# Two attention layers on one core: maxima of scores taken over two PSUM banks at once, scores in three single banks, and two of the three relative-position sets done as one

## The reference, cut to what matters

```python
# x: (16, 32, 32, 192) float32; 12 heads of 16; S = 32*32 = 1024
x = x + L0(_gn(x))     # _gn: group norm, 32 groups
x = x + L1(_gn(x))

def L0(x):             # global attention with decomposed relative positions
    q, k, v = split(x @ w_qkv.T + b_qkv)              # per head (S, 16)
    r_q = q.reshape(heads, H, W, 16)
    rel_h = einsum('bhwc,hkc->bhwk', r_q, Rh)         # Rh, Rw: (32, 32, 16)
    rel_w = einsum('bhwc,wkc->bhwk', r_q, Rw)
    bias = (rel_h[..., :, None] + rel_w[..., None, :]).reshape(heads, S, S)
    attn = softmax(q @ k.T * 16 ** -0.5 + bias)       # 1024 x 1024 per head
    return (attn @ v) @ w_proj.T + b_proj

def L1(x):             # 7x7 neighbourhood attention with 16 register keys
    scores = where(mask_cat, q @ concat(k, reg_k).T / 4, -1e30)
    return (softmax(scores) @ concat(v, reg_v)) @ out_w.T + out_b
```

## Time and profile before

| | |
|---|---|
| median of 3 runs | 4869.27 us (4869.14 to 4873.89) |
| profiled execution | 4862.39 us, span 4860.6 us |
| granted clock of TensorE, mean | 0.967 |
| TensorE busy | 4446.6 us, 91% of the span |
| VectorE busy | 3079.8 us, 63% |
| ScalarE busy | 2594.1 us, 53% |
| GpSimd busy | 892.4 us, 18% |

### The profile page before, as it was taken

One profiled execution on the slowest core, in us unless ns is written; L12 is line 12 of the kernel. 1 busy time (PEld: TensorE's weight loads), 2 busy tenths in 40 slices (PEclk: granted clock), 3 DMA queues, 4 the chain that ended last, 5 costly groups with the idle time before them and its releaser, 6 DMA issues.

```text
span 4860.6 us, 97545 instructions
## 1 busy us (share of the span) xinstructions
PE 4446.6 (91%) x32598; PEld 2268.6 (47%) x32598; DVE 3079.8 (63%) x5558; ACT 2594.1 (53%) x3955; POOL 892.4 (18%) x1901
## 2 busy tenths in 40 slices
PE   4879999999999999999999999999999999999988
PEld 3334453544535454453544535454453544535434
DVE  3736667666675756657566675756757566675644
ACT  1533556555564655555555565555546555565564
POOL 4122021222202222021222202222031221202111
PEclk7988999999999999999999999999999999999999
DMA  6333152442514433153442424433253432424402
GB/s 123 87 73 77 44 119 64 100 87 56 107 42 107 88 89 75 44 115 68 100 80 58 101 52 103 91 83 75 45 114 75 100 80 49 103 60 100 88 15 40
DMA packets 235869, 386.05 MB, mean 79 GB/s; under 512 B 58396, under 2 KB 133728, under 8 KB 235360
## 3 DMA queue, kind: packets, MB, share of 16 engines
q1 hardware_dynamic: 189280, 266.13, 23.7%
q10 hardware_dynamic: 21504, 75.51, 7.8%
q0 software_dynamic: 24576, 37.80, 4.9%
HBM read 227.79 MB, written 88.08 MB: 65 GB/s over the span
## 4 chain that ended last, share of the span: by engine, by line
PE 71%; DVE 11%; issue 6%; DMA 5%; SPq 5%; ACT 2%; DVEq 0%; ACTq 0%; POOL 0%
PE P L1143 14%; PE P L1161 13%; PE P L1102 12%; DVE mx L909 7%; PE P L966 5%; PE P L967 5%; PE P L1193 4%; PE P L1214 4%; DMA queries<-oraw 4%; PE P L1110 3%; PE P L1079 3%; SPq L514 3%; DVE mxc L915 2%; PE P L1186 1%; PE P L1231 1%
## 5 line engine op out<-in xcount | busy, mean ns | idle before, releaser
L909 DVE TENSOR_REDUCE mx<-P 128x1 f32<-128x512 f32 x3072 | 1921.3, 684 | 457.4 <-PE P L1102 453.3
L779 ACT ACTIVATE probs<-P 128x1024 f32<-128x1024 f32 x1536 | 1507.5, 1022 | 854.0 <-PE P L1161 853.8
L1102 PE MATMUL P<-K,AR 96*128 96x256 f16 x6144 | 1074.1, 278 | 56.6 <-DMA AR<-biases 29.5
L1161 PE MATMUL P<-AR,K 113*128 113x512 f16 x3072 | 924.9, 383 | 13.2 <-DMA AR<-mrow 12.6
L915 DVE TENSOR_REDUCE mxc<-P 128x1 f32<-128x336 f32 (+1 forms) x1536 | 656.3, 474 | 317.9 <-PE P L1111 315.0
L1143 PE MATMUL P<-probs,V 128*17 128x512 f32 x6144 | 813.5, 601 | 5.7 <-ACT probs L779 5.7
L1102 PEld LDWEIGHTS P<-K,AR 96*128 96x128 f16 x6144 | 532.2, 98 | 581.4 <-DVE mx L909 202.0
L795 ACT ACTIVATE probs<-P 128x320 f32<-128x320 f32 (+3 forms) x1632 | 612.1, 437 | 338.2 <-PE P L1214 268.4
L1161 PEld LDWEIGHTS P<-AR,K 113*128 113x128 f16 x3072 | 213.3, 98 | 670.3 <-ACT probs L779 519.6
L1110 PE MATMUL P<-K,A 112*128 112x320 f16 (+1 forms) x1536 | 405.2, 300 | 68.7 <-DVE mx L909 54.9
L1214 PE MATMUL P<-A,K 113*128 113x320 f16 (+2 forms) x1536 | 428.3, 300 | 14.7 <-ACT probs L795 14.3
(11 more groups left out here) (125 smaller groups left out, 3718.4 us busy)
## 6 DMA issues: line engine op xcount, KB each, us to landing
AR<-biases SPq DMA_DIRECT2D x384, 256.0 KB, 7.9
AR<-queries ACTq DMA_DIRECT2D x96, 512.0 KB, 5.9
biases<-xn SPq DMA_DIRECT2D x128, 256.0 KB, 2.6
AR<-queries ACTq DMA_DIRECT2D x96, 256.0 KB, 8.8
K<-oraw POOLq DMA_DIRECT2D x384, 64.0 KB, 4.7
xin<-in_x_dram SPq DMA_DIRECT2D x16, 768.0 KB, 10.5
queries<-oraw SPq DMA_DIRECT2D x384, 32.0 KB, 4.6
QA<-queries SPq DMA_DIRECT2D x192, 64.0 KB, 2.8
```

The costliest lines, as they stand in the source:

```text
L779: nc.scalar.activation(probs[:, u % RING, j:j + 2, :], P[:, b:b + 2, :], ACT.Exp).then_inc(p_done[0], 1)
L909: V_.reduce_max(mx[:, n // 2, n % 2:n % 2 + 1], bank, AX.X).then_inc(used, 1)
L1102: last = mm(bank[:, QD * (v % 2):QD * (v % 2) + QD], AR[0:ROWS_MAX[0], part % SLOTS, v, c, j, 128 * q:128 * q + 128], K0[0:ROWS_MAX[0], h, ...
L1161: last = mm(P[:, j, :], K0[0:ROWS, h, 128 * kt:128 * kt + 128], AR[0:ROWS, p % SLOTS, kt // 2, :, j, :], start=True, stop=True)
```

## The change

- L0 maxima in main0: a job is now a pair (`max2`): four matmuls into two neighbouring banks, one maximum over 1,024 columns, written straight to `mxc`; L912 and its semaphore are not used there. L1 maxima in main0 are pairs too: two tiles of equal width (`TILE_PAIRS`), one instruction with two results. In main1 they stay single.
- Job banks in main0: 3, 4, 5, 6 in place of 4, 5, 7. A pair takes two that begin at an even place of the ring; a transpose or stat takes one, and the next pair skips what is left of its two. Values go to bank 7.
- Scores in main0: three single banks; ScalarE takes each by itself (two exponentials of 512 in place of one of 1,024), and semaphores count singles.
- Relative positions: sets 1 and 2 are done together in main1 at steps 9 to 23 of every second step, eight jobs of 4 lines, two matmuls a line of 128 columns. Their parts are kept in `oraw` and `xin`, so ScalarE waits before it writes `oraw` again, and SP before it loads `xin`. Main0 has none. `QA` holds three sets; set 2's queries are fetched right behind set 1's.
- The wait for ones in row 96 of `xn` in L0's `out` is gone.

```diff
-RELS = 4
+RELS = 4, 8
-SCORES, JOBS = (4, 3), 3
-JOB_BANKS = ((4, 5, 7), (3, 4, 5))
+SCORES = 3
+JOB_BANKS, VALUES_BANK = ((3, 4, 5, 6), (3, 4, 5)), 7
+SINGLES = 2 * STEPS[0]
+TILE_PAIRS = ((0, 7), (1, 2), (3, 4), (5, 6))
...
+def max_pairs(layer, image, part):
+
+    return [("max2", layer, image, part, n) for n in range(0, ITEMS[layer] + 1, 2)]
...
-        before = jobs[len(jobs) - JOBS] if len(jobs) >= JOBS else None
-        after[place].append((len(jobs), job, before))
+        wide = 1 + (job[0] == "max2" and job[4] < ITEMS[job[1]])
+        at += at % wide
+        taken = [ring[(at + k) % len(ring)] for k in range(wide)]
+        before = max((held[b] for b in taken if b in held), default=None)
+        after[place].append((taken[0], job, None if before is None else jobs[before]))
+        for b in taken:
+            held[b] = len(jobs)
         jobs.append(job)
+        at += wide
...
-    placed += [(8 + 3 * n, job) for n, job in enumerate(rel_jobs(image, 2))]
...
-    placed += [(8 + 2 * n, job) for n, job in enumerate(rel_jobs(n0, 1))]
+    placed += [(9 + 2 * n, job) for n, job in enumerate(rel_jobs(n0, 1))]
...
                 query_blocks(im, 1)
+                query_blocks(im, 2)
...
                     fill_slot(image, part)
-                    if part == 2:
-                        query_blocks(image, 2)
...
+            def rel_moved():
+
+                while staged:
+                    image = staged.pop()
+                    for g in (1, 2):
+                        act.wait_ge(biases_out[g], (image + 1) * PER_BIASES)
...
-                        act.wait_ge(st_done[0], im * STEPS[0] + step + 1)
-                        b = 2 * (step % 2)
-                        nc.scalar.activation(probs[:, u % RING, j:j + 2, :], P[:, b:b + 2, :],
-                                             ACT.Exp).then_inc(p_done[0], 1)
+                        for k in range(2):
+                            single = 2 * step + k
+                            act.wait_ge(st_done[0], im * SINGLES + single + 1)
+                            nc.scalar.activation(probs[:, u % RING, j + k, :], P[:, single % SCORES, :],
+                                                 ACT.Exp).then_inc(p_done[0], 1)
...
+                        elif what == "max2" and layer == 0:
+                            V_.reduce_max(mxc[0][:, n // 2:n // 2 + 1], banks(at, 2), AX.X).then_inc(used, 2)
+                        elif what == "max2":
+                            (a, b), h = TILE_PAIRS[n % TT // 2], n // TT
+                            lo, hi = key_rows(a)
+                            V_.tensor_reduce(mxc[1][:, TT * h + a:TT * h + b + 1:b - a],
+                                             P[:, at:at + 2, 0:W * (hi - lo) + REG], AX.X, ALU.max).then_inc(used, 2)
...
+                    q = QA[:, sets[0]:sets[1], :, :].rearrange("p g h (l w) -> p (g h) l w", w=16)
+                    table, cols = n * lines // 16, 512 // lines
+                    for b in range(lines):
+                        line = n * lines % 16 + b
                         rhs = q[:, :, :, line] if table else q[:, :, line, :]
...
-                            last = mm(bank[:, 64 * b:64 * b + 64], lhs, rhs, start=(s == 0), stop=(s == 1))
+                            last = mm(bank[:, cols * b:cols * b + cols], lhs, rhs, start=(s == 0), stop=(s == 1))
...
                         for j in (2 * k, 2 * k + 1):
-                            h = GH * (p // 2) + j
-                            last = mm(P[:, j, :], K0[0:ROWS, h, 128 * kt:128 * kt + 128],
-                                      AR[0:ROWS, p % SLOTS, kt // 2, :, j, :], start=True, stop=True)
-                        last.then_inc(st_done[0], 1)
+                            h, single = GH * (p // 2) + j, 4 * u + j
+                            if single >= SCORES:
+                                pe.wait_ge(p_done[0], im * SINGLES + single - SCORES + 1)
+                            if single in (0, 2):
+                                banks_read(single // 2)
+                            mm(P[:, single % SCORES, :], K0[0:ROWS, h, 128 * kt:128 * kt + 128],
+                               AR[0:ROWS, p % SLOTS, kt // 2, :, j, :], start=True, stop=True).then_inc(st_done[0], 1)
```

More of the change, by code:

```diff
@@ L78, in max_jobs @@
     return [("max", layer, image, part, n) for n in range(ITEMS[layer] + 1)]
+def max_pairs(layer, image, part):
+    return [("max2", layer, image, part, n) for n in range(0, ITEMS[layer] + 1, 2)]
 def rel_jobs(image, g):
-    return [("rel", 0, image, g, n) for n in range(RELS)]
+    return [("rel", 0, image, g, n) for n in range(RELS[g])]
 def stat_jobs(layer, image):
@@ L104, in cost @@
 def cost(job):
-    return {"rel": 4, "stat": 1, "max": (7, 5)[job[1]]}[job[0]]
+    return {"rel": 4, "stat": 1, "max": (7, 5)[job[1]], "max2": (12, 9)[job[1]]}[job[0]]
 def evenly(jobs, first, end):
@@ L115, in evenly, with plan @@
     return placed
-def plan(steps, placed):
-    after, jobs = [[] for _ in range(steps)], []
+def plan(steps, placed, ring):
+    after, jobs, held, at = [[] for _ in range(steps)], [], {}, 0
     for place, job in sorted(placed, key=lambda p: p[0]):
@@ L386, in consumed, with rel_view @@
             if kind == "rel":
-                return rello_done, (image * G + part) * RELS + n + 1
+                return rello_done, image * sum(RELS) + part * RELS[0] + n + 1
             if kind == "stat":
                 return stat_used[layer], image * 2 + n + 1
-            return smax_used[layer], image * PER_ITEMS[layer] + part * (ITEMS[layer] + 1) + n + 1
-        def rel_view(bank, n, operand):
-            table, part = n // 2, 8 * (n % 2)
-            t = operand[table].rearrange("p h (l w) -> p h l w", w=16)
+            done = n + 1 + (kind == "max2" and n < ITEMS[layer])
+            return smax_used[layer], image * PER_ITEMS[layer] + part * (ITEMS[layer] + 1) + done
+        def rel_view(bank, n, operand, part):
+            lines, heads = 32 // RELS[part], GH * (part + 1)
+            table, first = n * lines // 16, n * lines % 16
+            t = operand[part][table].rearrange("p m (l w) -> p m l w", w=16)
             if table == 0:
-                return bank.rearrange("p (l h w) -> p h l w", l=8, h=GH), t[:, :, part:part + 8, :]
-            return bank.rearrange("p (w h l) -> p h l w", w=8, h=GH), t[:, :, :, part:part + 8]
+                return bank.rearrange("p (l m w) -> p m l w", l=lines, m=heads), t[:, :, first:first + lines, :]
+            return bank.rearrange("p (w m l) -> p m l w", w=lines, m=heads), t[:, :, :, first:first + lines]
         def rows_to_operands(queue, L, im, part, copies, done, take_wait=None):
@@ L523, in moves @@
                     fill_slot(image, part)
-                    if part == 2:
-                        query_blocks(image, 2)
                     if part == 1 and is_image(image, 0):
                         static_rows()
-                if what == "rel" and n == RELS - 1:
-                    biases_away(image, part)
-                if what == "max" and n == ITEMS[layer]:
+                if what == "rel" and n in (3, 7):
+                    biases_away(image, part, n)
+                if what in ("max", "max2") and n == ITEMS[layer]:
                     sp.wait_ge(*consumed(job))
@@ L771, in stage @@
                     rows_moved()
+                    rel_moved()
                 if kind == "main" and L == 0:
@@ L1046, in banks_read, with run_job @@
                     unread_qkv.clear()
-            def run_job(bank, job, before):
+            def run_job(at, job, before):
                 what, layer, image, part, n = job
+                bank = P[:, at, :]
                 if before:
@@ L1090, in run_job @@
                     pe.wait_ge(k_in[1][part], (image + 1) * PER_K)
+                tiles = [n + k for k in range(2 if what == "max2" else 1)]
                 if n == ITEMS[layer]:
-                    if layer == 0:
-                        pe.wait_ge(comb_done, image * PHASES[0] + part + 1)
+                    if layer == 0 and what == "max2":
+                        pe.wait_ge(*consumed(job[:4] + (n - 2,)))
+                        last = nc.tensor.transpose(bank[0:ITEMS[0] // 2, 0:128], mxc[0][:], ident[:])
+                    elif layer == 0:
+                        pe.wait_ge(comb_done, part + 1 if is_image(image, 0) else image * 2 + part)
@@ L1118, in run_jobs @@
                         banks_read(2)
-                        run_job(P[:, JOB_BANKS[L][at % JOBS], :], job, before)
+                        run_job(at, job, before)
             def jobs_read(after):
```

145 lines of the change are left out of this document (75 added, 70 removed).

## The result

The changed kernel takes 4917.8 us (4914.3 to 4918.9) against 4869.2 us before: ratio 1.0107, with a 95% interval of 1.0093 to 1.0121. It is 1.1% slower, where the forecast was 0.5% faster, and outside the forecast's range. The profiled execution has a span of 4912.5 us, 51.9 more than before.

What follows compares the result with a forecast made beforehand. TensorE's own work and waits were taken as the bound. Main0 -9.4 us 16 times, main1 +8.3 us 14 times and +9 for jobs ahead of the loop gave -25 us, 4844 us; range 4780 to 4905 with A's and B's.

Steps and rivals of the forecast that it cites:

- rival A: Position jobs: table 1 costs per matmul, not per column; 60 us less, 4784 us; chance 0.12.
- The wait for QA: Main1's first rel job of the second set also needs the third query block: +2.0 us; wait 4 to 5 us.
- The fourth score's cover: Main0: a unit's fourth score waits for the first's bank where ScalarE's exponential ends late; +2.0 us in all.
- rival B: Main0: the fourth score waits for the first exponential in all units; 60 us at 0.08 us each, 4904; chance 0.23.
- C: Main1: the longer QA wait costs more through late third block and lower clock; 27 us, 4871; chance 0.15.
- the 0.18 goes: Main0's full units: the second L0 group's bank wait vanishes in 14 units; with shorter units, -2.9 us per main0.
- waits sum to 6.7 us where they are 10.0 now: Main0 units with L0 and L1 pairs in both steps: shorter bank waits, -3.3 us.
- stat and other single jobs that break the pairing: Main0: after a single job the next pair takes the banks just used; two stat jobs cost +0.4 us.
- Rival D: Main0: mixed units keep their waits, two pairs being no deeper than three singles; 40 us, 4884; chance 0.08.
- The content: Main1's position jobs: table 0 +0.8 us, table 1 +3.74 us priced per column; sum +4.5 us.
- The wait of ScalarE for the biases ahead of `oraw`: Main1, step 30: ScalarE may not write oraw before the last pair tables left; bounds 0 and 1.9, taken +0.7 us.
- the clock: Main1: longer waits make half of the periods more run at the lower granted clock; +0.8 us.

Runs made afterwards that it cites:

- E2: The kernel before with position sets 1 and 2 done together in main1, main0's maxima and scores as before; 4933.9 us, ratio 1.0137.
- E7: The changed kernel with main0's maxima bank by bank instead of in pairs, over the four job banks; 4894.2 us, ratio 1.0074.
- E1: The changed kernel's main0 pairs and single score banks, with position sets as in the kernel before; 4873.0 us, ratio 1.0017.
- E15: E10 with banks split as before, four for main0's scores and three for its jobs; 4882.4 us, ratio 1.0043.
- E10: The kernel before with main0's scores in three single banks and four job banks, maxima single, position sets as before; 4801.6 us, ratio 0.9872.
- E8: The changed kernel with the eight jobs of sets 1 and 2 at steps 16 to 23 of main1; 4823.8 us, ratio 0.9927.
- E14: The kernel before with position set 1's four jobs in main1 at steps 16 to 22, not 8 to 14; 4837.5 us, ratio 0.9951.
- E5: The changed kernel with the second table's products reading queries in runs, each such matmul issued four times (values wrong); 4976.4 us, ratio 1.0234.
- E9: The changed kernel with main0's maxima as single banks and the eight set jobs at steps 16 to 23; 4814.9 us, ratio 0.9902.
- E13: E10 with position set 1's four jobs in main1 at steps 16 to 22, not 8 to 14; 4790.5 us, ratio 0.9860.
- E12: E11 with the query move and fill of phase 1 asked at step 28, as in both kernels; 4868.8 us, ratio 1.0018.
- E11: E9 with queries turned by VectorE so the second table reads runs, and phase 1's query move and fill at step 31; 4792.9 us, ratio 0.9864.

## Why the prediction was wrong

**Where it was right.** The maximum over two banks takes 1,221 ns (forecast 1,219). The second table's jobs cost by the column: 1.84 to 1.98 us start to start for eight matmuls of 128, so rival A, which I gave 0.12, didn't happen. No position job is left in main0, worth 5.7 us by E2 (forecast 4.7). The wait for QA ends 1.9 us later (forecast 2.0), though it is itself only 3.3 us long in the mean (I had named 4 to 5 as the sign). The fourth score's cover is short in some units, as I took it: 1.3 us in the seven units named at E7, against +2.0. Full units show no such wait, so rival B didn't happen. The two stages of jobs ahead of the loop cost 6.6 us more (forecast 9). Of the rivals, C was the right kind, but its 27 us were too few: by the stretch of main1 alone 47 us came on top of the sum.

**Main0: -9.4 forecast, -7.0 measured (-7.7 by the mean of the loop).** The steps that failed are the scores, banks and pairs, -4.7 in my sum against -1.4 (E2's main0 against the changed kernel's) or -0.75 (E1). First, "the 0.18 goes": only 0.09 of it did, in 15 units (not 14), 1.4 us. Second, the mixed units "waits sum to 6.7 us where they are 10.0 now": I compared two pairs with the three single banks of before and gave the pairs the gain. The gain is the fourth bank's with single results: 4.5 us in the ten mixed units from E2 to E7, 6.9 in all from E15 to E10; the pairs then take 2.8 (E7) to 4.4 (E10) of it back. Third, stat and other single jobs that break the pairing were put at +0.4; two stat units alone cost 3.96 each against 3.52 before, and a unit with the transpose behind them 3.62 against 2.92. Rival D named the mechanism and had 0.08.

**Main1: +8.3 forecast, +11.7 measured.** My sign "I am wrong if main0 is above 153 or main1 above 90" came as well: 153.1 and 91.0. The content, +4.5, agrees with the one comparison in which place and wait are nearly equal: E8 against E14 is 98.5 - 92.0 = 6.5 us, of which some 2 (an estimate: half of it) go with E8's 4.1 us more at the lower level. The wait of ScalarE for the biases ahead of `oraw`, +0.7 in the sum, was nothing here (one wait of 0.06 us). The step that failed is the clock, +0.8. I priced it as the aftermath of a longer wait; the low-clock time rose by 14 us a period, most of it where TensorE was busy. With 4.5 for the content, 1.9 for the wait and my 0.3 for the ring, which no run measured, 5.0 of the 11.7 us are left for the clock; 14 us at half speed could cost 7 at most. E5 shows that with strided columns it falls where it does not with runs of the same length, E8 that the place behind the wait makes it worse: without that wait main1 is 6.5 us shorter, 2.9 of it the wait itself (49.1 to 8.3 us in 14 periods). The rule that I cited from the Trainium skill (TensorE: Matmul & The Clock Gate, "What's actually happening") is about an idle array. In this trace the clock fell as well with the array busy by the profile (3.78 to 4.00 of 4 us).

**The balance.** Both errors point the same way. By the means, the 16 main0s gave 119 us where the sum had 150, and the 14 main1s cost 163 us where it had 116: 31 + 47 = 78 us, which is the distance from -25 to +52 but for 1. The loop's turn (+5), the jobs ahead of the loop (-2 against the sum) and the stages behind it (-3) cancel. The direction failed because the sum was a small difference between two large terms (-150 and +125), and each had a mechanism on the losing side to which I gave too little. Neither "the change is bad" nor "it is good" survives. The fourth job bank is worth 1.7% (E15 to E10). The pairs cost 0.3% (E7, E9) without position jobs in main0 and 1.5% with them (E10 against E1). Moving the sets costs 1.4% where they were put (E2), and 0.3 to 0.4% when they stand behind the arrival of their queries (E9 against E10 and E13).

## What to carry to other kernels

Try an extra bank with single results before you pair results. Here a pair halved the number of instructions, but it needed two neighbours free at once and waited for the whole of the longer reader, and every odd job between pairs broke the rotation. Place a job behind the arrival of what it reads, and look at the first job of the kind: here 94 us hung on one number in a list. When you shorten a stage, look for the moves that it will now issue earlier, and into which other move's way: in E5 the slow step had kept two transfers apart.

## What the runs showed of the hardware that was not expected

TensorE's granted clock fell to the lower level, 0.50 to 0.52 over 8 us, while the profile showed the engine busy, around jobs whose matmuls read a moving operand of single f16 elements 32 bytes apart; jobs of the same length that read runs kept 1.00 (E5). It is not so of every such job. In the main0 of the kernel before, with two of them, 5 of 15 periods have low-clock time; in the changed kernel, E2 and E7, with no position job in main0, none has.

Such a matmul of 128 columns takes 0.23 us start to start at either level, while one that reads runs takes 0.055 us at the higher and 0.107 at the lower (medians of L1121 in the changed kernel). So the strided job's own time doesn't show the clock; its neighbours' does.

Two moves of 256 and 512 KB, issued on ScalarE's queue within half a microsecond of a 256 KB move on SyncE's, went with a landing of that move after 7.2 us in place of 2.8 (E12 and E11). In E12 the DMA share was 0.97 to 1.08 in the 8 us behind.
